# A bound on the gathers in flight: each waits for the landing of the one two places ahead

## The chip, the cores and the metric

The kernel runs on one core of a Trainium2 chip. The metric is the device time of one execution in microseconds (us); less is better. The core's engines each run an instruction stream of their own: PE (TensorE, with PEld for its weight loads), DVE (VectorE), ACT (ScalarE), POOL (GpSimd) and SP (SyncE), which here only issues DMAs. They meet on semaphores.

## The reference, cut to what matters

Four layers run one after another on a stream of 4 images of 48 x 48 tokens with 128 channels. The change lies in layer 1, a deformable convolution: each token looks at nine taps, each at a place that is computed from the data, and each tap is a weighted sum of four neighbouring tokens.

```python
offsets = conv3x3(x_normalized, offset_w) + offset_b          # 2 x 9 per token
y0, x0 = floor(py), floor(px); wy, wx = py - y0, px - x0        # py, px: place of each tap
val = (gather(y0, x0) * (1 - wy) * (1 - wx) + gather(y0, x0 + 1) * (1 - wy) * wx
       + gather(y0 + 1, x0) * wy * (1 - wx) + gather(y0 + 1, x0 + 1) * wy * wx)
out = einsum('bhwkc,kcf->bhwf', val, kernel.reshape(9, C, F)) + bias
```

Layer 2 (linear attention, then a choice of two among eight experts), layer 0 ahead of them (a selective scan) and layer 3 behind (attention, spectral filters) are not touched.

## The kernel before

`layers12` runs layer 1 for all four images and, woven into it, layer 2 for the first images: while the tiles of one image are convolved, the image before it goes through attention and the one before that through the experts. The stream lies in SBUF; an image is `TB` = 18 tiles of 128 tokens, and there are `NTILE` = 72 tiles.

For each image a table in HBM, `neighbours_b`, holds for every place the four neighbouring tokens side by side, 512 floats a row. SP stores these rows (line 991) when PE and ACT have turned an image's normalized channels into tokens, eight DMAs in each of eight of an image's 18 tile times, one image ahead of their use; so in the tile times of the first three images. DVE makes the row numbers `idx` of all 18 x 9 taps of an image at once (line 1055).

The path of one tile n is this. POOL issues nine indirect DMAs (line 1249), one for each tap (`TAPS` = 9): each takes 128 rows of 2 KB, 256 KB, into `G[:, g]`, where `g = n % GB` is one of `GB` = 3 buffers. POOL issues the nine of a tile in a row, without looking at their landing. Ahead of a tile's first gather it waits for `s_bank`: PE must have used the buffer up, three tiles earlier; ahead of an image's first it also waits for the table and the row numbers. Each gather adds 16 to the one semaphore of its buffer, `s_gat[g]`, when it lands. DVE (`weight`, line 1092) waits until all nine of the tile have landed, then multiplies `G` with the corner weights in two parts, three taps and six. PE (`turn`, line 1297) turns the 36 blocks and adds up the four corners of each tap, ACT copies the sums out of PSUM (line 1422), and PE (`convolve`, line 1315) multiplies them with the kernel.

The order is written by hand, tile by tile, the same on each engine. In the turn of tile n, DVE weighs the first part of tile n + 1, does its share of preparing the next image, then a round of layer 2, then the second part of tile n + 1 and a second round. PE turns tile n, lays a round of layer 2, convolves tile n and lays a second round. POOL has nothing but the gathers in this stage.

Of the kernel before, what the change touches and what calls it, by code (L numbers as in the profile page):

```python
# [840 lines left out]
TAPS = 9  # L841
IW = WW + 4
GB = 3
# [11 lines left out]
def layers12(nc, x_in, w, wa, wm, tables):  # L855

    with ExitStack() as ctx:
# [3 lines left out]
        sem = Semaphores(nc, ctx, "l12_")  # L861
# [43 lines left out]
        s_bank, s_wd, s_ev, s_out, s_res, s_wp = (sem(n) for n in (  # L905
            "sum_bank", "weighted", "summed_copied", "out_made", "residual", "weights_spread"))
        s_xs = [sem(f"rows_stored_{r}") for r in range(XR)]
        s_gat = [sem(f"gathered_{r}") for r in range(GB)]
        s_lp, s_ld, s_hp, s_hd, s_sq, s_ln, s_rs, s_kb, s_kn, s_ke, s_qn, s_qe, s_vs, s_mx, s_e, s_st, s_wc, s_dl, s_dr, s_cm = (sem(n) for n in (
            "round_laid", "round_taken", "half_laid", "half_weighted", "squared", "log_var", "rstd", "k_biased", "k_negative", "k_exp",  # L910
            "q_negative", "q_exp", "quotient_step", "logits_centred", "logits_exp", "choice_step", "mix_weights", "den_log", "den_inverse", "centring_made"))
# [44 lines left out]
        with nc.Block() as block:  # L956
# [38 lines left out]
            def _(dve):  # L995
# [77 lines left out]
                def spread(b, half):  # L1073
                    a, f = (t[:, half * HT:(half + 1) * HT].rearrange("p n (k t) -> p n k t", t=2) for t in (near, far))
                    dve.wait_ge(s_idx, b + 1)
                    if b or half:
                        dve.wait_ge(s_wd, 2 * (b * TB + half * HT))
                    for q in range(4):
                        dve.tensor_tensor(W4[:, :, :, q:q + 1], (f, a)[q // 2][:, :, :, 0:1], (f, a)[q % 2][:, :, :, 1:2],
                                          ALU.mult).then_inc(s_wp, 1)  # L1080

                def weight(n, part):

                    g = n % GB
                    if part == 0:
                        if n % HT == 0:
                            spread(n // TB, n // HT % 2)
                            dve.wait_ge(s_wp, 4 * (n // HT + 1))
                        dve.wait_ge(s_gat[g], (n // GB + 1) * TAPS * 16)
                    taps = (tap_banks[0], range(3, TAPS))[part]  # L1090
                    cols = slice(4 * taps[0], 4 * taps[-1] + 4)
                    dve.tensor_tensor(G[:, g, cols], G[:, g, cols],  # L1092
                                      W4[:, n % HT].rearrange("p k q -> p (k q)")[:, cols].unsqueeze(2).broadcast_to([P, 4 * len(taps), C]),
                                      ALU.mult).then_inc(s_wd, 1)
# [121 lines left out]
                for part in range(2):  # L1216
                    weight(0, part)
                dve.wait_ge(s_w2, 16 * len(loads2))
                dve.tensor_tensor(cmat[:], ident[:], ones_c[:], ALU.subtract).then_inc(s_cm, 1)
                for n in range(NTILE):  # L1220
                    k = 2 * (n - TB)
                    if n + 1 < NTILE:
                        weight(n + 1, 0)
                    if n // TB + 1 < NB:
                        prepare(n // TB + 1, n % TB)
                    if n >= TB:
                        take(k)
                        weigh_half(k)
                    if n + 1 < NTILE:
                        weight(n + 1, 1)  # L1230
                    if n >= TB:
                        take(k + 1)
                        weigh_half(k + 1)
                take(NRD - 1)

            @block.gpsimd
            def _(pool):
                for n in range(NTILE):
                    b, g = n // TB, n % GB
                    if n == 0:  # L1240
                        pool.wait_ge(s_zd, 16 * 16 * NB)
                    if n % TB == 0:
                        for r in range(XR):
                            pool.wait_ge(s_xs[r], 16 * 8 * len(range(r, (b + 1) * NPR, XR)))
                        pool.wait_ge(s_idx, b + 1)
                    if n >= GB:
                        pool.wait_ge(s_bank, NBK * (n - GB + 1))
                    for k in range(TAPS):
                        pool.indirect_dma_start(out=G[:, g, 4 * k:4 * k + 4, :].rearrange("p q c -> p (q c)"), out_offset=None,  # L1249
                                                in_=tables[b], in_offset=bass.IndirectOffsetOnAxis(ap=idx[:, b % 2, n % TB, k:k + 1], axis=0),  # L1250
                                                ).then_inc(s_gat[g], 16)

            @block.tensor
            def _(pe):
# [1432 lines left out]
def program(nc, w, x_in, out, scratch):  # L2687

    with nc.sbuf_tensor("eps", [P, 2], F32) as eps, nc.semaphore("eps_loaded") as s_eps, \
            nc.psum_tensor("psum", [P, 8 * BANK], F32) as psum:  # L2690
        with nc.Block() as block:
            @block.sync
            def _(sp):
                sp.dma_start(eps[:], w["eps"]).then_inc(s_eps, 16)
                sp.wait_ge(s_eps, 16)

        def part(prefix):

            own = {k[len(prefix):]: v for k, v in w.items() if k.startswith(prefix)}
            return {**w, **own, "eps5": eps[:, 0:1], "psum": psum}  # L2700

        x1, _, _, f_scr = scratch
        c_rows = nc.dram_tensor("c_rows", (2, NS, RC), F32, kind="Internal").ap()
        back_rows = nc.dram_tensor("back_rows", (KD // 2, NRC, KEPT, RC), F32, kind="Internal").ap()
        layer0(nc, x_in, part("l0_"), x1, c_rows, back_rows)

        with nc.sbuf_tensor("stream", [P, NT], F32) as stream:
            w["stream"] = stream
            tables = [nc.dram_tensor(f"neighbours_{b}", (QW * QW, 4 * C), F32, kind="Internal").ap() for b in range(NB)]
            layers12(nc, x1, part("l1_"), part("la_"), part("mo_"), tables)  # L2710
            layer2_attention(nc, part("la_"), NB - 1)
            layer2_experts(nc, part("mo_"), (NB - 2, NB - 1))
            layer3_attention(nc, part("ca_"))
            f_sum = nc.dram_tensor("filter_sums", (2, KF * 2, SETS * SETW), F16, kind="Internal").ap()
            layer3_spectral(nc, part("st_"), f_scr, f_sum.rearrange("o k (g x) -> o k g x", g=SETS), out)
# [24 lines left out]
```

## Time and profile before

| | us |
|---|---|
| runs, median of 3 (least, most) | 7853.32 (7848.3, 7858.25) |
| the profiled execution | 7834.9 |
| its span, first to last instruction | 7833.1 |
| from the first gather's issue to DVE's start on the last tile | 3915.05 to 4786.21 |

The profile is of one execution; its numbers add up to its own span, which is 0.2% under the median of the runs. Busy time is what an engine's instructions take; the time that an instruction of POOL takes to issue a DMA is counted as busy there, the transfer is not. A wait is put down to what came true last. "Landing" of a DMA is counted from the start of its issue.

### The profile page before, as it was taken

The numbers are of one execution on the slowest core, as the hardware profiler recorded it, in microseconds if no ns is written. First come the engines' busy times: TensorE is split into PE (matmuls) and PEld (weight loads), VectorE is DVE, ScalarE is ACT, GpSimd is POOL, SyncE is SP. The second block draws the span as 40 slices with busy tenths as digits, with TensorE's granted clock in tenths as the row PEclk, the third lists the DMA queues.
The fourth block names the chain that finished last, engine by engine and source line by source line (L and its number), as shares of the span: only waits on it lengthen the run. The fifth ranks groups of instructions, "written<-read, shape, count | busy, mean of one in ns | idle before, by whom it ended". The sixth has DMA issues, their size and how long they took to land. (4 is left out here: it accounts for less than half of the span.)

```text
span 7833.1 us, 167005 instructions
## 1 busy us (share of the span) xinstructions
PE 6962.2 (89%) x61178; PEld 6072.3 (78%) x61178; DVE 5887.2 (75%) x8892; ACT 4277.6 (55%) x9069; POOL 3533.3 (45%) x2869
## 2 busy tenths in 40 slices
PE   8999899998999989999668998899789889899898
PEld 6888678886788867888468785466588888889888
DVE  7899888997889978899557775555566666666666
ACT  6888678985789848898313332254522222222222
POOL 5888558884688837888277663200000000000000
PEclk9999999999999999999789999899899999999999
DMA  2333223332233313333377763000033333333333
GB/s 67 94 96 98 76 69 94 96 96 64 81 93 97 96 53 93 91 99 97 111 232 232 203 192 91 3 1 0 9 117 114 112 111 111 118 111 111 101 111 99
DMA packets 593198, 771.58 MB, mean 99 GB/s; under 512 B 51175, under 2 KB 530536, under 8 KB 590225
## 3 DMA queue, kind: packets, MB, share of 16 engines
q1 hardware_dynamic: 540561, 590.63, 25.3%
q0 software_dynamic: 51840, 169.91, 7.4%
q8 instruction: 551, 9.03, 0.5%
q14 instruction: 246, 2.02, 0.1%
HBM read 724.84 MB, written 35.50 MB: 97 GB/s over the span
## 5 line engine op out<-in xcount | busy, mean ns | idle before, releaser
L684 POOL TENSOR_TENSOR l_arena<-l_arena 128x768 f32<-128x768 f32 x1536 | 2574.3, 1687 | 490.1 <-DVE l_arena L614 399.6
L614 DVE TENSOR_TENSOR_SCAN l_arena<-l_arena,psum 128x772 f32<-128x772 f32 x1536 | 2647.6, 1748 | 169.5 <-PE psum L440 142.3
L535 ACT ACTIVATE l_arena<-l_arena,l_A 128x384 f32<-128x384 f32 x3072 | 1652.2, 602 | 2.1 <-DVE l_arena L584 2.1
L440 PE MATMUL psum<-l_arena 128*128 128x128 f32 x9216 | 1219.8, 283 | 154.6 <-DVE l_arena L614 145.4
L440 PEld LDWEIGHTS psum<-l_arena 128*128 128x128 f32 x9216 | 1111.8, 195 | 302.6 <-issue 287.9
L451 PE MATMUL psum<-l_ident,l_arena 128*128 128x128 f32 x9216 | 1267.7, 274 | 69.6 <-ACT l_yT L541 43.2
L451 PEld LDWEIGHTS psum<-l_ident,l_arena 128*128 128x128 f32 x9216 | 1060.6, 142 | 90.7 <-issue 53.2
L525 ACT ACTIVATE l_arena<-l_arena,l_BT 128x256 f32<-128x256 f32 x2304 | 997.0, 496 | 50.9 <-PE psum L438 37.8
L2307 POOL TENSOR_TENSOR st_mab<-st_xr 128x384 f32<-128x384 f32 x8 | 7.8, 998 | 2214.0 <-DVE st_xr L2297 2214.0
L2582 ACT ACTIVATE st_own_s<-psum 128x384 f32<-128x384 f32 x256 | 125.5, 490 | 1315.3 <-PE psum L2419 1194.8
L1249 POOL DMA_INDIRECT l_G<-neighbours,l_idx x648 | 620.7, 958 | 390.9 <-issue 189.5
L438 PE MATMUL psum<-l_ident,l_arena 128*128 128x128 f32 x4608 | 639.0, 275 | 0.9
L2419 PE MATMUL psum<-st_FS,st_xt 128*128 128x128 f16 x6912 | 536.4, 222 | 95.7 <-issue 94.4
L438 PEld LDWEIGHTS psum<-l_ident,l_arena 128*128 128x128 f32 x4608 | 523.4, 141 | 94.2 <-issue 55.4
L2419 PEld LDWEIGHTS psum<-st_FS,st_xt 128*128 128x128 f16 x6912 | 448.6, 99 | 117.9 <-issue 100.7
L2409 PE MATMUL psum<-st_F,st_xt 128*128 128x128 f16 x4608 | 434.0, 221 | 56.5 <-issue 56.5
L2439 PE MATMUL psum<-st_Uc,st_Wm 128*128 128x128 f32 (+1 forms) x2560 | 463.9, 313 | 6.4 <-DVE st_Uc L2559 6.4
L1092 DVE TENSOR_TENSOR l_G<-l_G,psum 128x1536 f32<-128x1536 f32 (+1 forms) x144 | 366.2, 2547 | 116.5 <-DMA l_G<-neighbours,l_idx 116.0
L591 DVE TENSOR_TENSOR l_arena<-psum,l_BT 128x384 f32<-128x384 f32 x768 | 409.8, 534 | 0.0
L1297 PE MATMUL psum<-l_ident,l_G 128*128 128x128 f32 x2592 | 317.6, 283 | 65.0 <-DVE l_G L1092 37.5
L2439 PEld LDWEIGHTS psum<-st_Uc,st_Wm 128*128 128x128 f32 x2560 | 364.2, 196 | 7.5 <-DVE st_Uc L2559 7.5
L1297 PEld LDWEIGHTS psum<-l_ident,l_G 128*128 128x128 f32 x2592 | 302.1, 146 | 87.6 <-DVE l_G L1092 43.6
(435 smaller groups left out, 10950.0 us busy)
## 6 DMA issues: line engine op xcount, KB each, us to landing
st_FS<-filter_sums SPq DMA_DIRECT2D x128, 1155.0 KB, 9.1
l_arena<-c_rows SPq DMA_DIRECT2D x768, 192.0 KB, 3.0
l_arena<-back_rows SPq DMA_DIRECT2D x768, 192.0 KB, 3.1
st_F<-filter_parts SPq DMA_DIRECT2D x128, 320.5 KB, 6.8
neighbours<-l_xt SPq DMA_DIRECT2D x256, 72.0 KB
st_mab<-in_st_mp SPq DMA_DIRECT2D x68, 256.0 KB, 9.2
st_mab<-in_st_mm SPq DMA_DIRECT2D x68, 256.0 KB, 6.8
l_G<-neighbours,l_idx POOLq DMA_INDIRECT x648, 3.7
```

The costliest lines, as they stand in the source:

```text
L438: mm = pe.transpose(ps[:, o:o + P], xT[:, rank[s] % 2, t, h * P:(h + 1) * P], ident[:])
L440: mm = pe.matmul(ps[:, o:o + P], dtuT[:, g % 2, t, h * P:(h + 1) * P], diagB[:, rank[s] % 3, t, :], start=True, stop=True)
L451: mm = pe.matmul(y_ps[:, t, h * P:(h + 1) * P], hC[:, s % NHC, h, t * P:(t + 1) * P], ident[:], start=(n == 0 and h == 0 and t % 2 == 0), ...
L525: ins = act.activation(xT[:, i % 2, t, :], dtuT[:, g % 2, t, :], ACT.Copy, scale=BT[:, g % 2, t, n:n + 1])
L535: act.activation(decay[:, s % NDC, half(h)], dtv[:, g % 2, h, :], ACT.Exp, scale=A[:, g // NRC, h, n:n + 1]).then_inc(s_exp, 1)
L614: dve.tensor_tensor_scan(hbuf[:, n, run], decay[:, s % NDC, run], x2_ps[s % 2][:, run], 0.0, ALU.mult, ALU.add).then_inc(s_scan, 1)
L684: pool.tensor_tensor(hC[:, s % NHC], halves(hbuf[:, s % NS, :]), Cs[:, s % NCS, :].unsqueeze(1).broadcast_to([P, 2, RC]), ALU.mult).then_i ...
L1249: pool.indirect_dma_start(out=G[:, g, 4 * k:4 * k + 4, :].rearrange("p q c -> p (q c)"), out_offset=None, in_=tables[b], in_offset=bass.In ...
L1297: mm = pe.matmul(bank(i % 2, P * a, P * (a + 1)), G[:, g, 4 * k + q, :], ident[:], start=(q == 0), stop=(q == 3), is_transpose=True, skip_ ...
L2409: mm = pe.matmul(ps[:, LOW + i * P:LOW + (i + 1) * P], xt[:, xpart, blk, :], tap[:, r, fpart, z, shift + at:shift + at + P], start=(n + m ...
L2419: mm = pe.matmul(ps[:, at + i * P:at + (i + 1) * P], xt[:, xpart, x0 + LB - 1 - i, :], FS[:, r, fpart, z, three, shift + i * P:shift + (i ...
L2439: mm = pe.matmul(ps[:, o:o + hi - lo], Wm[:, r, z, m, :], src[:, lo - c * RC:hi - c * RC], start=False, stop=False, skip_group_check=True)
```

## The change

The nine gathers of a tile are split by parity over two semaphores: the taps 0, 2, 4, 6, 8 of a buffer add to `s_gat[g][0]`, the taps 1, 3, 5, 7 to `s_gat[g][1]`. Ahead of tap k, from the third on, POOL waits until tap k - 2 has landed. The first two taps of a tile wait for no landing, as before. DVE's weighting of a tile now waits for both semaphores of the buffer, each at its own count (five gathers and four). The order of the instructions on all engines stays; three more semaphores are cleared at the end of the stage.

```diff
-        s_gat = [sem(f"gathered_{r}") for r in range(GB)]
+        s_gat = [[sem(f"gathered_{r}_{e}") for e in range(2)] for r in range(GB)]
+        OF_TILE = (TAPS - TAPS // 2, TAPS // 2)
...
-                        dve.wait_ge(s_gat[g], (n // GB + 1) * TAPS * 16)
+                        for e in range(2):
+                            dve.wait_ge(s_gat[g][e], (n // GB + 1) * OF_TILE[e] * 16)
...
                     for k in range(TAPS):
+                        if k >= 2:
+                            pool.wait_ge(s_gat[g][k % 2], (n // GB * OF_TILE[k % 2] + k // 2) * 16)
                         pool.indirect_dma_start(out=G[:, g, 4 * k:4 * k + 4, :].rearrange("p q c -> p (q c)"), out_offset=None,
                                                 in_=tables[b], in_offset=bass.IndirectOffsetOnAxis(ap=idx[:, b % 2, n % TB, k:k + 1], axis=0),
-                                                ).then_inc(s_gat[g], 16)
+                                                ).then_inc(s_gat[g][k % 2], 16)
```

On POOL, the start of the stage before: 27 gathers of three tiles with one wait at their head, then the first gather of the fourth tile, which waits for PE (`l12_sum_bank`), and eight more.

```order
L1236 UNCONDITIONAL_BRANCH [waits barrier_Pool_Activation_PE_DVE_SP_gather]
L1249 DMA l_G<-neighbours,l_idx 128x512 [waits l12_rows_stored_2,l12_rows_stored_1,l12_indices_made,l12_rows_stored_0,l12_border_zeroed]
L1249 DMA l_G<-neighbours,l_idx 128x512 x26
L1249 DMA l_G<-neighbours,l_idx 128x512 [waits l12_sum_bank]
L1249 DMA l_G<-neighbours,l_idx 128x512 x8
```

The same place now (`l12_gathered_0_1` is buffer 0, odd taps), the first tile's last two gathers and on into the second tile; the rows left out by "..." go on in the same alternation:

```order
L1253 DMA l_G<-neighbours,l_idx 128x512 [waits l12_rows_stored_2,l12_rows_stored_1,l12_indices_made,l12_rows_stored_0,l12_border_zeroed]
L1253 DMA l_G<-neighbours,l_idx 128x512
L1253 DMA l_G<-neighbours,l_idx 128x512 [waits l12_gathered_0_0]
L1253 DMA l_G<-neighbours,l_idx 128x512 [waits l12_gathered_0_1]
...
L1253 DMA l_G<-neighbours,l_idx 128x512 x2
L1253 DMA l_G<-neighbours,l_idx 128x512 [waits l12_gathered_1_0]
L1253 DMA l_G<-neighbours,l_idx 128x512 [waits l12_gathered_1_1]
```

No gather has moved; seven of a tile's nine have a wait that they hadn't, and the two that follow each other without one (`x2`) are the first two of the next tile.

On DVE, at the third and fourth tile, before: the weighting of a tile's first three taps waits for the buffer's one semaphore.

```order
L1092 TENSOR_TENSOR l_G<-l_G,psum 128x1536 [waits l12_gathered_2]
L1010 COPY l_gst<-psum 128x2 [waits l12_gn_group]
L1011 TENSOR_TENSOR l_gst<-l_gst 128x1 [waits l12_dve_a]
L1012 TENSOR_TENSOR l_gst<-l_gst 128x1 [waits l12_dve_a]
L1092 TENSOR_TENSOR l_G<-l_G,psum 128x3072
L1092 TENSOR_TENSOR l_G<-l_G,psum 128x1536 [waits l12_gathered_0]
```

And now:

```order
L1094 TENSOR_TENSOR l_G<-l_G,psum 128x1536 [waits l12_gathered_2_1,l12_gathered_2_0]
L1011 COPY l_gst<-psum 128x2 [waits l12_gn_group]
L1012 TENSOR_TENSOR l_gst<-l_gst 128x1 [waits l12_dve_a]
L1013 TENSOR_TENSOR l_gst<-l_gst 128x1 [waits l12_dve_a]
L1094 TENSOR_TENSOR l_G<-l_G,psum 128x3072
L1094 TENSOR_TENSOR l_G<-l_G,psum 128x1536 [waits l12_gathered_0_1,l12_gathered_0_0]
```

The instructions stand as they stood; the first part of each weighting waits for two semaphores in place of one.

## Rows read from the trace of the kernel before

**Rows 1.** The page's busy times, and POOL in 40 slices of the span.

```profile
PE 6962.2 (89%) x61178; PEld 6072.3 (78%) x61178; DVE 5887.2 (75%) x8892; ACT 4277.6 (55%) x9069; POOL 3533.3 (45%) x2869
POOL 5888558884688837888277663200000000000000
```

**Rows 2.** Busy time by stretch (us): stretch, length, engines, clock, DMA share, GB/s.

```profile
3770.00:3914.00 144.00, 82.09 (x272) 46.69 (x272) 67.31 (x121) 24.23 (x37) 1.86 (x2) 0.69 0.39 122
3914.00:4136.00 222.00, 152.11 (x1108) 140.76 (x1109) 118.58 (x102) 37.40 (x82) 167.64 (x176) 0.85 0.78 227
4136.00:4352.00 216.00, 194.32 (x1406) 176.40 (x1404) 159.31 (x227) 80.78 (x206) 163.60 (x171) 0.96 0.78 229
4352.00:4570.00 218.00, 214.04 (x1432) 178.19 (x1432) 159.78 (x244) 75.88 (x201) 140.18 (x146) 0.98 0.69 198
4570.00:4800.00 230.00, 228.24 (x1597) 192.44 (x1596) 162.21 (x226) 70.25 (x180) 149.31 (x157) 1.00 0.63 182
```

**Rows 3.** Waits, 3914 to 4790: us in total, times, longest.

```profile
POOL l_G L1249 <- issue: 189.5, 622, 0.3
...
DVE l_G L1092 <- DMA l_G<-neighbours,l_idx: 116.0, 29, 14.0
POOL l_G L1249 <- PE psum L1297: 58.2, 25, 4.6
```

**Rows 4.** Timeline, 3913.8 to 3918: start, length, operation, [idle before, releaser].

```profile
3913.91 0.25 DVE L1055 CAST l_idx<-l_low 128x162 uint32<-128x162 f32 x1
...
3915.05 1.15 POOL L1249 DMA_INDIRECT l_G<-neighbours,l_idx  x1 [143.19 <-DVE l_idx L1055]
3916.51 0.95 POOL L1249 DMA_INDIRECT l_G<-neighbours,l_idx  x1 [0.30 <-issue]
3917.76 0.95 POOL L1249 DMA_INDIRECT l_G<-neighbours,l_idx  x1 [0.30 <-issue]
```

**Rows 5.** Line 1092 alone in the third stretch: DVE's busy time (instructions).

```profile
4352.00:4570.00 218.00, 79.80 (x32) 0.98 0.69 198
```

**Rows 6.** Line 1249, whole stage: ns min/median/max, starts; then landing times, us.

```profile
L1249 POOL DMA_INDIRECT l_G<-neighbours,l_idx x648: 940/946/2398, 3915.1 to 4782.5; - x162
...
DMA to landing us min/median/max: 3.1/3.7/5.2
```

**Rows 7.** Timelines of POOL, PE and ACT about 4420, a tile that waits for PE.

```profile
4418.84 0.94 POOL L1249 DMA_INDIRECT l_G<-neighbours,l_idx  x1 [0.30 <-issue]
4420.07 4.09 PE L1297 MATMUL psum<-l_ident,l_G 128*128 128x128 f32 x36
4424.20 0.49 ACT L1422 ACTIVATE l_val<-psum 128x384 f32<-128x384 f32 x1 [0.82 <-PE psum L1297]
4424.43 0.94 POOL L1249 DMA_INDIRECT l_G<-neighbours,l_idx  x1 [4.65 <-PE psum L1297]
```

**Rows 8.** Line 1249: one lone, nine after rest, nine with stores, first stretch.

```profile
L1249 POOL DMA_INDIRECT l_G<-neighbours,l_idx x1: 940/940/940, 4424.4 to 4424.4; - x1
...
DMA to landing us min/median/max: 3.4/3.4/3.4
L1249 POOL DMA_INDIRECT l_G<-neighbours,l_idx x9: 942/946/948, 4700.6 to 4710.6; - x9
...
DMA to landing us min/median/max: 3.3/3.6/3.8
L1249 POOL DMA_INDIRECT l_G<-neighbours,l_idx x9: 946/946/1160, 4200.0 to 4210.3; - x9
...
DMA to landing us min/median/max: 3.6/4.4/5.0
DMA to landing us min/median/max: 3.4/3.8/5.2
```

**Rows 9.** DVE's timeline at the end of the stage.

```profile
4786.21 1.75 DVE L1092 TENSOR_TENSOR l_G<-l_G,psum 128x1536 f32<-128x1536 f32 x1 [1.53 <-DMA l_G<-neighbours,l_idx]
4789.09 0.29 DVE L1177 TENSOR_TENSOR stream<-stream,psum 128x128 f32<-128x128 f32 x1 [1.12 <-PE psum L1344]
...
4809.95 0.27 DVE L1579 MEMSET la_vv<- 128x258 f32 x1 [3.93 <-PEq L55]
```

## The prediction

> **What bounds the kernel now.** The change lies in one stage, so I first looked for what paces that stage. The totals of the page and its slices say little of it: over the whole span PE is busy 89% and POOL 45%, and POOL's busy slices from the 20th to the 25th are the stage of layers 1 and 2 [rows 1]. The busy time by stretch, one stretch for each image, says more [rows 2]. In the first two stretches POOL is busy 167.64 of 222 us and 163.60 of 216 us, and PE only 152.11 and 194.32. To POOL's busy time its own gaps are to be added: in the waits of the stage, 622 of the 648 gathers have "issue" time ahead of them, 189.5 us in all, 0.30 us each [rows 3]. 176 gathers of 0.95 us and as many gaps of 0.30 make 220 of the first stretch's 222 us: POOL issues without a pause there, 1.25 us from one gather to the next [rows 4], 11.25 us for a tile of nine. In the third and fourth stretch POOL rests, 58.2 us in all, until PE has used up a buffer [rows 3], and PE is busy 214 of 218 and 228 of 230 us [rows 2]: PE paces those. The 32 weightings of the third stretch [rows 5], two a tile, make 16 tiles of 13.6 us. Over all 72 tiles the stage runs from 3915.05, its first gather, to 4786.21, when DVE gets the last one [rows 4, 9]. That is 12.1 us a tile.
>
> Then I asked how long one gather takes from its issue to its landing, since the change makes that a link of a chain. The line's own answer gives 3.1 / 3.7 / 5.2 us as least, median and greatest [rows 6]. At one issue each 1.25 us, 3.7 us means that about three gathers are in flight now (3.7 / 1.25 = 2.96). Two is therefore fewer than the kernel uses at present, on the very engine that paces half of the stage.
>
> **The change part by part.**
>
> *The semaphores.* Three more of them are cleared behind the stage. Between DVE's last operation there and its first in the next stage lie 3.93 us of idle time [rows 9], which hold the clearing of the stage's semaphores among other things (51 instructions in the program's order); three more can cost at most 3 x 3.93 / 51 = 0.2 us. DVE's second wait per tile comes true before or with the first, because the ninth gather, the last to be issued, counts on the semaphore that DVE waits for first. Its price is under the 0.04 us by which an engine starts after its releaser (ACT, below), on an engine that has idle time at each tile. I book both as nothing, 0.2 us if I am wrong.
>
> *The waits on POOL.* Gathers 3 to 9 of each tile wait for the landing of the gather two places ahead, 7 x 72 = 504 waits. Queued behind the waiting instruction is all of POOL's later work, which in this stage is gathers alone; SP's stores of neighbour rows stand in another queue. Who waits for POOL is DVE's weighting of the tile, and behind DVE the PE transposes; DVE's waits for gathers are 116.0 us now [rows 3], and they are what will grow.
>
> The length of a link is the time to landing, L, and the step from the landing to the next issue, h. No row shows a POOL instruction released by a landing. The nearest show it released by PE: a tile's 36 transposes run from 4420.07 for 4.09 us, to 4424.16; ACT, waiting for the same, starts at 4424.20, POOL at 4424.43 [rows 7]. So h is 0.27 on POOL, where ACT needs 0.04. It is also the 0.30 of the gap between gathers, so I read it as POOL's own start-up, paid after the release. The other end is the first gather of the stage, 0.89 us after the cast that it waited for ended (3914.16 to 3915.05, [rows 4]); that is one start after 143 us of rest with several waits. I take 0.28.
>
> For L there are four rows. A gather that POOL issued after 4.65 us of rest, when the gathers ahead had landed, took 3.4 [rows 7, 8]. Of nine issued from 4700.6 on, behind a shorter rest, the fastest took 3.3, the median 3.6 [rows 8]. The least of all is 3.1 [rows 6]. Where SP stores rows the median of nine is 4.4 [rows 8]; that touches 8 of 18 tiles in three images. With two in flight a gather is less alone than the 3.4 and less crowded than the median of 3.7, so I take 3.55, midway, and keep 3.1 and the 3.8 of the crowded first stretch [rows 8] as ends.
>
> The odd-numbered gathers carry the tile: gathers 1, 3, 5, 7 and 9 follow each other at L + h = 3.83 us. The even ones start 1.25 us behind and reach no further (1.25 + 3 x 3.83 = 12.74 for the eighth, and 1.25 more is 13.99, before the ninth's 15.32). The next tile's first gather waits for no landing, so it follows the ninth at 1.25. The pace of a tile becomes 4 x 3.83 + 1.25 = **16.57 us** in place of 11.25.
>
> That is above the 13.6 us of a PE-paced tile, so the gathers set the pace in all 72 tiles, and a wait for a free buffer goes away (the three buffers are then used up long before they are wanted). Of the 5.32 us that a tile gains, what the PE-paced stretches already took is not paid again; I therefore sum by end times, not by adding to each tile. The last tile's first gather starts at 3915.05 + 71 x 16.57 = 5091.5, its ninth 15.3 later at 5106.8, and it lands at 5110.4. Now DVE gets it at 4786.2 [rows 9]. Difference: **+324 us**. Behind it the tail is the same work, less the 1.12 us that DVE there waits for a PE that is late [rows 9] and then isn't. Sum: +323 us.
>
> The profiled execution took 7834.9 us (span 7833.1), the median of the runs is 7853.3, 0.2% more. I add the sum to the median: **8176 us**; on the profiled run it would be 8158.
>
> Ends: L = 3.1 gives 14.77 us a tile and +193 by the same sum, L = 3.8 gives 17.57 and +395. That is 8046 to 8249.
>
> A rule that speaks of L, in sentences that the sum does not need. The rows show the landing to depend on what else moves: 3.4 us alone, 4.4 among SP's stores [rows 8]. The Trainium skill, "DMA: Bandwidth & Descriptors", section "Latency and other measured facts", says that less load on HBM makes the fixed part of a DMA smaller. By the rows alone the sum is +323; by that rule it would go towards the +193 of the least landing, since two gathers load less than three.
>
> **The rivals.**
>
> *Not slower: the landings get short enough.* What must hold is a tile of 12.1 us, the stage's present mean: (12.1 - 1.25) / 4 - 0.28 = 2.43 us for L. Then the pauses on POOL only fill what it rests now for buffers, and the time stays at 7853. For it speaks that a third of the traffic in flight goes; the stage's DMA share is 0.63 to 0.78 [rows 2], so queues may stand. Against it speaks the lone gather, 3.4 us with nothing ahead of it, and that not one of the recorded landings is under 3.1. Chance 2%. Anything faster than before needs an L below that and a gain besides; 1%.
>
> *The landings shrink to between 2.5 and 3.1 us.* A weaker form of the same: 2.5 gives 12.37 us a tile, +20 and 7873; 2.6 gives 12.77, +49 and 7902; 3.1 ends at 8046. It takes a landing faster than any recorded. Chance 5%. (The Trainium skill, same page, "Anatomy of one DMA — SWDGE (gpsimd) path", fits a DMA as 2.0 us and its bytes over 436 GB/s; for a gather's 256 KB that is an estimate of 2.6 us. The lone gather's 3.4 us [rows 8] agrees only if the 0.95 us of issuing come on top, which makes 3.55.)
>
> *Slow starts on POOL.* If a start after a landing costs 0.89 rather than 0.28, a tile takes 4 x 4.44 + 1.25 = 19.0 us, the sum is +499 and the time 8352. Against it: POOL started 0.27 us after its releaser from a rest of 4.65 us [rows 7], and the new rests are shorter than that. Chance 5%, and 3% for landings that stay above 3.8 for another reason (stores that spread).
>
> *PE's clock becomes the bound.* PE rests more, and the granted clock could fall: it was 0.85, a mean between its levels of 1.2 and 2.4 GHz, in the stretch where PE was busy 69% [rows 2]. In the third stretch PE has 214.04 / 16 = 13.4 us a tile at 0.98; it would take over from 16.57 at a clock of 0.79. PE would still be busy about 80%, more than where 0.85 was granted, so I don't expect it. At 0.69, the lowest of the stretch before the stage [rows 2], those 16 tiles would take 19.0 us, +39 us, 8215. Chance 3%, and inside the range.
>
> **How the numbers follow.** The forecast, gathers as the pace of all tiles with L between 3.1 and 3.8, has 81%. The range 8046 to 8250 holds it and the clock's case, 84% in all; the other four rivals and a time under 7837 make the 16% outside. Measurements of this kernel tell 0.2%, some 16 us, from no change: faster 1%, within that 2%, slower 97%.
>
> **What would show it.** POOL's starts of line 1253 in pairs, 1.25 to 1.5 us and then about 2.4 us, with 3.83 us from one to the next but one; a tile's first gathers 16.57 us apart in all four images; POOL's waits for PE gone and waits for landings in their place, some 2.3 us for every second gather; DVE's wait for gathers at about 72 x 5 us; PE's busy share under 80% in the stage. The rest of the kernel, before 3915 and behind the stage, should be the same to a microsecond. Wrong would be: landings under 2.5 us, or starts on POOL that come 0.9 us behind a landing.

## The result, and the profile after

The changed kernel took 8165.87 us (median of 4 runs, 8156.31 to 8166.18), the kernel before 7851.43 in the runs beside it: a ratio of 1.0396, 95% interval 1.0378 to 1.0414. That is 314 us slower; 8176 was forecast, and the forecast range was 8046 to 8250. The profiled execution took 8166.18 us, its span is 8164.4.

The busy time by stretch answers to [rows 2], again one stretch for each image (stretch, length, then PE, PEld, DVE, ACT and POOL busy, granted clock, DMA share, GB/s):

```profile
3916.00:4213.00 297.00, 165.49 (x1044) 152.86 (x1044) 108.30 (x89) 35.55 (x78) 155.11 (x163) 0.76 0.57 159
4213.00:4514.00 301.00, 212.01 (x1352) 194.96 (x1352) 150.09 (x208) 79.29 (x200) 154.97 (x163) 0.84 0.56 158
4514.00:4816.00 302.00, 256.60 (x1609) 212.44 (x1610) 176.80 (x272) 82.49 (x215) 155.34 (x162) 0.90 0.56 157
4816.00:5110.00 294.00, 236.59 (x1480) 192.96 (x1478) 153.37 (x214) 67.39 (x172) 153.68 (x163) 0.91 0.51 146
```

From each image's first gather to the next one's, the four images took 204.5, 205.5, 239.0 and 218.5 us before (the last one up to its last gather), the first two paced by POOL and the others by PE. The stretches of [rows 2] are cut a little otherwise, the first two hold 176 and 171 gathers in place of 162. Counted the same way the images now take 296.6, 301.0, 302.7 and 289.9 us, whatever else they hold: one thing paces them all. POOL's busy time is what it was, some 155 us an image on the mean, so POOL issues the same work with longer rests. The traffic fell from 227 to 159 GB/s in the first stretch.

What the rests are is said by the gathers' own line, which answers to [rows 3, 6] (the idle time of POOL ahead of the line by what ended it, in us and times; then who waited for the line; then landing times):

```profile
L1253 POOL DMA_INDIRECT l_G<-neighbours,l_idx x648: 940/944/2369, 3916.1 to 5106.3; - x162
its engine sat idle before it (us, times) until:
  DMA l_G<-neighbours,l_idx: 502.4, 458
  DVE l_idx L1056: 143.4, 1
  issue: 68.2, 184
  PE psum L1301: 1.5, 5
who waited for it (us, times):
  DVE l_G L1094: 561.9, 72
...
DMA to landing us min/median/max: 3.1/3.4/6.2
```

POOL's waits for a free buffer, 58.2 us before, are 1.5 us now: the buffers lie ready. In their place stand 502.4 us of waits for landings. DVE waits for every one of the 72 tiles. And the landing itself has become quicker at the median, 3.4 us for 3.7, with fewer gathers side by side.

The chain is seen gather by gather in POOL's timeline of the first tile, which answers to [rows 4]:

```profile
3916.10 1.15 POOL L1253 DMA_INDIRECT l_G<-neighbours,l_idx  x1 [143.36 <-DVE l_idx L1056]
3917.56 0.95 POOL L1253 DMA_INDIRECT l_G<-neighbours,l_idx  x1 [0.30 <-issue]
3919.78 0.94 POOL L1253 DMA_INDIRECT l_G<-neighbours,l_idx  x1 [1.27 <-DMA l_G<-neighbours,l_idx]
3921.09 0.94 POOL L1253 DMA_INDIRECT l_G<-neighbours,l_idx  x1 [0.37 <-DMA l_G<-neighbours,l_idx]
3923.29 0.94 POOL L1253 DMA_INDIRECT l_G<-neighbours,l_idx  x1 [1.26 <-DMA l_G<-neighbours,l_idx]
...
3930.47 0.94 POOL L1253 DMA_INDIRECT l_G<-neighbours,l_idx  x1 [1.27 <-DMA l_G<-neighbours,l_idx]
3931.72 0.95 POOL L1253 DMA_INDIRECT l_G<-neighbours,l_idx  x1 [0.30 <-issue]
3932.97 0.95 POOL L1253 DMA_INDIRECT l_G<-neighbours,l_idx  x1 [0.30 <-issue]
```

The third gather starts 3.68 us after the first, the fifth 3.51 after the third, the ninth 14.37 after the first, and the next tile's first two follow at 1.25 us each without a wait. From the first gather to the last one's start, 3916.1 to 5106.3, lie 72 tiles less that last step, so a tile takes (1190.2 + 1.25) / 72 = 16.55 us, and a link of the chain (16.55 - 1.25) / 4 = 3.82.

The end of the stage on DVE answers to [rows 9]:

```profile
5109.58 1.75 DVE L1094 TENSOR_TENSOR l_G<-l_G,psum 128x1536 f32<-128x1536 f32 x1 [9.13 <-DMA l_G<-neighbours,l_idx]
5111.25 0.28 DVE L1179 TENSOR_TENSOR stream<-stream,psum 128x128 f32<-128x128 f32 x1
...
5131.75 0.27 DVE L1583 MEMSET la_vv<- 128x258 f32 x1 [4.43 <-PEq L55]
```

From the first gather to DVE's start on the last tile the stage takes 1193.5 us, 871.2 before: +322.3. The tail behind it takes 22.2 us for 23.7. The stretch from there to the end took 3032.7 us and 3023.2 in the two profiled executions; in the run with the semaphores split and no wait (below), where that code is the same, it took 3037. So the spans' difference of 331 us is 321 from the stage and its tail, 1 ahead of it, and the rest is how executions differ behind it.

### The profile page after: what moved, and what is told of

It reads as the page before. It is cut to its first block and busy times, and to the rows that moved or that the text cites. A ratio compares the mean times of both kernels' runs of the same rounds, so it can differ in the third digit from the quotient of the medians.

```text
span 8164.4 us, 167068 instructions
## 1 busy us (share of the span) xinstructions
PE 7063.5 (87%) x61174; PEld 6150.2 (75%) x61178; DVE 5886.7 (72%) x8892; ACT 4281.8 (52%) x9069; POOL 3532.0 (43%) x2869
## 3 DMA queue, kind: packets, MB, share of 16 engines
q0 software_dynamic: 51840, 169.91, 7.4%
## 5 line engine op out<-in xcount | busy, mean ns | idle before, releaser
L1253 POOL DMA_INDIRECT l_G<-neighbours,l_idx x648 | 619.1, 955 | 715.4 <-DMA l_G<-neighbours,l_idx 502.4
L1094 DVE TENSOR_TENSOR l_G<-l_G,psum 128x1536 f32<-128x1536 f32 (+1 forms) x144 | 366.7, 2550 | 562.2 <-DMA l_G<-neighbours,l_idx 561.9
L1301 PE MATMUL psum<-l_ident,l_G 128*128 128x128 f32 x2592 | 343.8, 297 | 108.5 <-DVE l_G L1094 79.5
L1301 PEld LDWEIGHTS psum<-l_ident,l_G 128*128 128x128 f32 x2592 | 329.4, 156 | 138.5 <-DVE l_G L1094 87.4
```

What stands on the lines that cost most here:

```text
L1301: mm = pe.matmul(bank(i % 2, P * a, P * (a + 1)), G[:, g, 4 * k + q, :], ident[:], start=(q == 0), stop=(q == 3), is_transpose=True, skip_ ...
```

## The experiments

Theory: the landing time is now a link of a chain, and a tile takes four links and one issue. Rival 1: each of the 504 waits costs POOL a fixed time, 314 / 504 = 0.62 us. Rival 2: it is the split of the semaphores, and DVE's second wait.

**The split alone.**

```diff
-                        if k >= 2:
-                            pool.wait_ge(s_gat[g][k % 2], (n // GB * OF_TILE[k % 2] + k // 2) * 16)
```

> The two semaphores a buffer and DVE's two waits stay, POOL's 504 waits are taken out. Theory (the chain of landings paces the gathers: a tile takes 4 links of landing time plus start, 4 x 3.83 + 1.25 us): without the chain the time is that of the kernel before, 7851 within 16 us. Rival 1 (each wait on POOL costs about 314 / 504 = 0.62 us whatever it waits for): 7851 too. Rival 2 (the split of the semaphores and DVE's second wait cost the time): stays at 8166.

Measured: 7859.82 us beside 7846.55, ratio 1.0013 (1.0003 to 1.0023). POOL's rests in that run are those of [rows 3], 189.5 us of issue and 58.3 us for PE. Rival 2 falls, for all but 0.1%. Most of that tenth lies outside the stage: from its first gather to its last the profiled executions take 868.4 us here and 867.5 before. What the rest is stays open. By its design this run can't tell rival 1 from the theory; the next two can.

**One in flight.** One semaphore a buffer, and each gather waits for the one ahead of it:

```diff
-                        if k >= 2:
-                            pool.wait_ge(s_gat[g][k % 2], (n // GB * OF_TILE[k % 2] + k // 2) * 16)
+                        if k >= 1:
+                            pool.wait_ge(s_gat[g][k % 1], (n // GB * OF_TILE[k % 1] + k // 1) * 16)
```

> Each gather of a tile waits for the one ahead of it, one semaphore a buffer. Theory: eight links of 3.35 + 0.28 and one issue of 1.25 make 30.3 us a tile; over 71 tiles and the last one's nine gathers the stage ends 1312 us later than before: about 9160. Rival 1: 576 waits at 0.62 us, +357, 8208.

Measured: 9163.16 us, one run. Rival 1 is out by 955 us. POOL's timeline in the middle of the stage shows single links, and below it the landing times of the run:

```profile
4501.19 0.94 POOL L1253 DMA_INDIRECT l_G<-neighbours,l_idx  x1 [2.56 <-DMA l_G<-neighbours,l_idx]
4504.76 0.94 POOL L1253 DMA_INDIRECT l_G<-neighbours,l_idx  x1 [2.63 <-DMA l_G<-neighbours,l_idx]
4508.38 0.95 POOL L1253 DMA_INDIRECT l_G<-neighbours,l_idx  x1 [2.68 <-DMA l_G<-neighbours,l_idx]
4511.94 0.95 POOL L1253 DMA_INDIRECT l_G<-neighbours,l_idx  x1 [2.61 <-DMA l_G<-neighbours,l_idx]
...
DMA to landing us min/median/max: 3.2/3.3/4.5
```

Starts lie 3.57, 3.62 and 3.56 us apart, the median landing is 3.3. Taken gather by gather from the trace, POOL starts 0.26 us after the landing that it waited for (570 waits, 0.258 to 0.260), as it did after PE [rows 7], and not 0.89 as at the stage's first start. The sum, 9160, is 3 us off.

**Three in flight.** Three semaphores a buffer, and each gather waits for the one three places ahead:

```diff
-                        if k >= 2:
-                            pool.wait_ge(s_gat[g][k % 2], (n // GB * OF_TILE[k % 2] + k // 2) * 16)
+                        if k >= 3:
+                            pool.wait_ge(s_gat[g][k % 3], (n // GB * OF_TILE[k % 3] + k // 3) * 16)
```

> Each gather waits for the one three places ahead in its tile, on three semaphores in turn: 432 waits in place of 504. Theory: gathers 1, 4, 7 make a chain of two links of 3.7 + 0.28 = 3.98 us where three issues take 3.75, so a tile goes from 11.25 to about 11.7 us, paid only in the two image times that POOL paces, 36 tiles: about 16 us more than before, 7867, and some more where rows are stored; under 7900. Rival 1 (0.62 us for each wait): 432 x 0.62 = 268 us, 8119.

Measured: 7903.49 us beside 7846.55, ratio 1.0068 (1.0051 to 1.0085): +57 us. Rival 1's 8119 is out here too. The theory's sign is right, its size isn't: 16 us were expected, and under 7900. The gathers' line says where the rest is:

```profile
its engine sat idle before it (us, times) until:
  DMA l_G<-neighbours,l_idx: 169.0, 280
...
DMA to landing us min/median/max: 3.1/3.7/7.8
```

From image to image the stage grew by 29, 31, 0 and 5 us. So the wait is paid where the theory had it, in the two images that POOL paces, but at 1.6 to 1.7 us a tile. Two links at the median, 2 x (3.7 + 0.28), are only 0.46 us over the six issues between, but 280 of the 432 waits held POOL up, for 0.6 us each. Without a bound, a landing of 5 us delays nothing as long as the tile's last one isn't late. With three there is no slack at all (3.98 against 3.75 us), so a slow landing holds up what follows, and a quick one afterwards gives nothing back. I had reckoned with the median. The mean landing of these two images, 4.0 us, gives 1.06 us a tile by the same sum, 38 us in all. That the rest comes from the spread too, since POOL issues the three chains in one order and a late landing in one holds up the others, is the likely reading; no run shows it apart.

**The bound over the tile's edge.** In the changed kernel the first two gathers of a tile wait for no landing; here they do:

```diff
+                        elif n:
+                            pool.wait_ge(s_gat[(n - 1) % GB][1 - k], ((n - 1) // GB + 1) * OF_TILE[1 - k] * 16)
```

> As the changed kernel, but the first two gathers of a tile wait for the last two but one place of the tile ahead too: never more than two in flight. Theory: nine links make two tiles, 4.5 links a tile in place of 4 and an issue of 1.25; at 3.4 + 0.28 that is 16.56 us a tile, at 3.6 + 0.28 (rows stored) 17.46: 0 to 64 us above the changed kernel, about 8185. The first gather's landing, 3.5 us and more in the changed kernel, comes down to that of the others, 3.4. Rival 1: 142 waits more at 0.62 us, +88, 8254.

Measured: 8223.96 us (8213.53 to 8229.79), ratio to before 1.0473 (1.0456 to 1.0491), 58 us above the changed kernel. From first to last start its 647 steps take 1.92 us each, 3.84 a link and 17.28 a tile, 0.73 more than the changed kernel: 71 x 0.73 = 52. That is the upper half of what the theory gave, and 30 us under rival 1's. A tile's first two gathers land after 3.3 and 3.4 us at the median, where they took 3.6 and 3.7 in the changed kernel: that much of their landing came from the crowd at the tile's edge.

**No later stores.** SP stores the first image's rows alone, before the stage's first gather:

```diff
-                for b in range(NB):
+                for b in range(1):
                     for m in range(NPR):
...
-                            pool.wait_ge(s_xs[r], 16 * 8 * len(range(r, (b + 1) * NPR, XR)))
+                            pool.wait_ge(s_xs[r], 16 * 8 * len(range(r, NPR, XR)))
...
-                                                in_=tables[b], in_offset=...
+                                                in_=tables[0], in_offset=...
...
-                        act.wait_ge(s_xs[g % XR], 16 * 8 * (g // XR))
+                        act.wait_ge(s_xs[g % XR], 16 * 8 * min(g // XR, len(range(g % XR, NPR, XR))))
```

> The changed kernel, but SP stores neighbour rows of the first image alone, ahead of the stage's gathers, and all 72 tiles take their rows from that table; so the output is that of other rows for three images. The 24 tiles that had stores beside them in the changed kernel have none. Theory (landing times pace, and what stretches them is SP's stores): every tile goes at the pace of those that had none, 15.8 us in the changed kernel's trace, in place of 16.56 on the mean: 71 x 0.76 = 54 us less, 8112. Rival (the pace does not hang on what else the DMA engines do): 8166.

Measured: 8147.75 us (8146.79 to 8149.99), beside 8173.98 for the changed kernel and 7845.16 for the kernel before on the same chip:

> The changed kernel once more, on the chip of the two runs beside it: 8166 within 16 us by every theory.

That is 26 us less, half of the 54 expected. Stores do stretch the chain (a tile takes 16.13 us for 16.56), but not all of its slow tiles go with them. Tiles of 17 to 19 us remain, among others at the places 23, 34, 40, 66 and 67 in both kernels. The 54 was also too much from the start. In the changed kernel's trace 15.8 us is the pace of the tiles that have neither stores nor, as the next run brings up, a packet of instructions beside them. All its 47 tiles without stores took 16.18 us on the mean, the 24 with stores 17.31; those 24 x 1.13 = 27 us are about what went.

**Mirrored rows.** The run before, with one edit:

```diff
-                                                ...IndirectOffsetOnAxis(ap=idx[:, b % 2, n % TB, k:k + 1], axis=0),
+                                                ...IndirectOffsetOnAxis(ap=idx[:, b % 2, TB - 1 - n % TB, k:k + 1], axis=0),
```

> The run without later stores, with the tiles of an image taking their rows in the opposite order (tile 18b + s gathers what tile 18b + 17 - s gathered), so the output differs once more. In the traces of the changed kernel and without later stores the tiles 23, 34, 40, 66 and 67 (from 0) are slow in every run, 17.3 to 19 us against a median near 16. Theory A (the rows that they ask for are slow to read): the slow tiles move to their mirror places 30, 19, 49, 59 and 58. Theory B (something else at that place of the program, such as fetches of instructions that use the same DMA engines): they stay where they are. The time is that of the run without later stores, 8148 within 16 us, by both.

Measured: 8144.57 us, one run. The slow tiles stayed: 18.85 us at place 23, 17.54 at 40, 17.23 at 66 and 18.35 at 67 (34 fell to 16.69), and their mirror places 19, 30, 49 and 58 took 15.4 to 16.4. The fifth mirror place, 59, took 17.17, but 17.09 before the mirroring too. So it is not the rows. POOL's timeline of tile 67, and then the DMA queues in its 18.35 us and in the 15.6 us of the tile behind it (packets, MB, share of 16 engines):

```profile
5001.09 0.95 POOL L1253 DMA_INDIRECT l_G<-neighbours,l_idx  x1 [0.30 <-issue]
5002.34 0.95 POOL L1253 DMA_INDIRECT l_G<-neighbours,l_idx  x1 [0.30 <-issue]
5004.86 0.94 POOL L1253 DMA_INDIRECT l_G<-neighbours,l_idx  x1 [1.57 <-DMA l_G<-neighbours,l_idx]
5007.15 0.94 POOL L1253 DMA_INDIRECT l_G<-neighbours,l_idx  x1 [1.35 <-DMA l_G<-neighbours,l_idx]
5009.86 0.95 POOL L1253 DMA_INDIRECT l_G<-neighbours,l_idx  x1 [1.76 <-issue]
...
q0 software_dynamic: 720, 2.36, 43.4%
q8 instruction: 1, 0.02, 0.5%
q14 instruction: 1, 0.01, 0.1%
...
q0 software_dynamic: 720, 2.36, 51.6%
```

The slow tile has packets of the queues named instruction in it, the quick one has none. Counted the same way for the 71 tiles that another follows, from one tile's first gather to the next one's: 28 tiles without a packet of queue q8 take 15.7 us on the mean, 43 with one take 16.35. In the run without later stores it is 28 at 15.8 and 43 at 16.4. Those 43 x 0.6 = 26 us are what was missing from the expected 54. In part POOL itself stands: the 1.76 us ahead of the fifth gather are put down to nothing that the profile shows. Such stands come at fixed places, eleven tiles apart: ahead of the sixth gather of tile 12 and of the fifth of tiles 23, 34, 45, 56 and 67, in every run with two in flight. Three of them in the run without later stores (tiles 23, 34 and 56):

```profile
4304.07 0.94 POOL L1253 DMA_INDIRECT l_G<-neighbours,l_idx  x1 [2.75 <-issue]
...
4482.59 0.94 POOL L1253 DMA_INDIRECT l_G<-neighbours,l_idx  x1 [2.59 <-issue]
...
4837.68 0.94 POOL L1253 DMA_INDIRECT l_G<-neighbours,l_idx  x1 [2.81 <-issue]
```

With one in flight they are 4.05 to 4.85 us long; before the change and with the split alone no gap put down to "issue" is over 0.3. Besides, in the tiles 4, 22 and 40 the issue of a gather or two takes 1.5 to 2.8 us in place of 0.95, before the change as after it. In the run without later stores eight of the 43 tiles with a packet have such a stand or such an issue and take 17.6 us on the mean, the other 35 take 16.1. So some 14 of the 26 us lie in the tiles where POOL stands, the rest in small parts in the others. That the packets cause both, the slow landings and the stands, is argued from their meeting in the same tiles; no run took them away, and why POOL stands at these places stays open.

**Half rows.** Gathers of 1 KB a row:

```diff
-                        pool.indirect_dma_start(out=G[:, g, 4 * k:4 * k + 4, :]..., 
-                                                in_=tables[b], ...
+                        pool.indirect_dma_start(out=G[:, g, 4 * k:4 * k + 2, :]...,
+                                                in_=tables[b].rearrange("r (h c) -> (r h) c", h=2), ...
```

> The changed kernel with gathers of 1 KB a row in place of 2 KB: two of each tap's four neighbours, and from other rows, so the output differs; the other half of the buffer is set to zero once at the start of the stage. The packets of a gather took 14.3 us of engine time in the trace of before (7.4% of 16 engines' span over 648 gathers), 0.9 us on 16 engines. Theory with the landing made of bytes in good part: 0.45 us less a link, 4 x 0.45 = 1.8 us a tile, 8166 - 127 = 8039. Rival (the landing is a fixed time, bytes hardly count): 8166, or up to 14 us more for the zeroing.

Measured: 7979.09 us (7978.24 to 7988.43), 195 us under the changed kernel beside it, more than either side expected.

```profile
L1254 POOL DMA_INDIRECT l_G<-neighbours,l_idx x648: 940/944/1854, 3915.7 to 4921.6; - x162
...
DMA to landing us min/median/max: 2.5/2.8/4.7
```

The issue takes the same 944 ns, the landing 2.8 us for 3.4. A tile takes (1005.9 + 1.25) / 72 = 13.99 us, 2.57 less, 0.64 a link. So the landing isn't a fixed time: half the bytes are worth 0.64 us, where the packets' time on the DMA engines gave 0.45. That two gathers share the engines explains little of it, since a gather of 2 KB rows alone in flight still takes 3.3 us. With the bytes the packets are fewer too (the gathers' queue has 31104 for 51840, and 84.98 MB for 169.91), and the rows lie elsewhere; the run does not tell bytes from packets.

## Why the prediction was right, point by point

- **What bounds the stage.** Right. The chain paces all four images alike, and the waits for a free buffer went, 58.2 to 1.5 us. The 13.6 us of a PE-paced tile came from a stretch that isn't quite an image; the third image took 239.0 / 18 = 13.3. Nothing hung on it.
- **The link.** 3.83 us foreseen, 3.82 measured; the tile 16.57 and 16.55; the stage +324 and +322.3; the tail -1.1 and -1.5. The start after a landing, read from a start after PE as 0.28, is 0.26 in the runs with one and with two in flight. The step from PE as a releaser to a DMA as one was the least sure of the sum, and it held.
- **The landing, 3.55 us.** Right on the mean, by a wrong picture, so in good part by luck. I took one value between lone and crowded. What came is 3.3 to 3.4 us for most gathers, so that a tile without stores or instruction packets takes about 15.8 us, and a tail up to 6.2 us that pulls the mean up: gathers behind a tile's edge, where up to four are in flight, gathers beside stores, and tiles with instruction packets. Two of the three, and POOL's own stands, I had not counted or named. The rule of the Trainium skill, "DMA: Bandwidth & Descriptors", section "Latency and other measured facts", that a lighter load makes the fixed part smaller, agrees with the median, 3.7 to 3.4 us; its consequence, a time well under the sum, did not come, because the tail stayed.
- **The even gathers reach no further.** Right as a rule, but they start mostly 1.3 to 1.6 us behind, not 1.25, and once in 72 tiles the ninth gather follows the eighth at once instead of waiting for the seventh's landing.
- **Split semaphores, nothing.** 0.13% (0.03 to 0.23), at the bound of what can be told. The idle time behind the stage that holds the clearing went from 3.93 to 4.43 us, with the split alone as well: 0.5 us for three semaphores, where I had put 0.2 as the most.
- **What would show it.** POOL's rests were foreseen as 2.3 us for every second gather; they are about 1.3 and 0.5 us in turn. The 2.3 was a slip: the steps of about 2.4 us beside it leave 1.45 behind an issue of 0.95. DVE's waits were put at 360 us and are 561.9: DVE's waits in the stage that PE ended fell from 129.6 to 14.1 us, and that time now ends with a landing. PE was to be busy under 80%: over the stage it is 73%, in the third stretch 85%. The code behind the stage was to take the same to a microsecond; it took 9.5 us more, and 13.8 more with the split alone, so it can't be told that well.
- **The clock.** That rival went some of the way: the granted clock, a mean between the levels of 1.2 and 2.4 GHz, fell from 0.98 to 0.90 in the third stretch and from 0.85 to 0.76 in the first, where PE rested most. PE still had 45 us to spare in the third. With POOL's waits for PE at 1.5 us it cost the stage nothing that shows.
- **Not slower.** It needed landings of 2.43 us; only with half the bytes did they come near, 2.8, and even then the time was 1.0175 times that of before.

The terms erred by 1 to 2 us, and the sum by 10: 8176 for 8166. The difference is of the size by which this kernel's executions differ outside the stage. On the chip of the last experiments the same two kernels lie 329 us apart (8173.98 and 7845.16, ratio 1.0416), so the +323 stands between the two measurements, 314 and 329.

## What to carry to other kernels

A bound on transfers in flight turns each landing into a link of a chain. Its price is read from three rows: the landing time of a lone transfer, the engine's start after a release, and the pace of issue now. If the bound times the pace of issue is less than landing plus start, the chain paces, and the sum is to be made with the mean landing, not the median: with a tight bound slow landings are paid and quick ones give nothing back. Where the bound just balances landing plus start, even the mean gives too little (three in flight cost 57 us where the median gave 16 and the mean 38). Sum it by the end times of the stage, so that what another engine paced there isn't counted twice.

## What the runs showed of the hardware

- A gather's landing hangs on its bytes, or on the packets that go with them, more than the packets' time says: 128 KB less made a link 0.64 us shorter, about 200 GB/s within one gather. The Trainium skill, "DMA: Bandwidth & Descriptors", section "Anatomy of one DMA — SWDGE (gpsimd) path", has bytes over 436 GB/s, which would be an estimate of 0.30 us for the half; the measurement decides, for gathers of 1 and 2 KB rows.
- Packets of the instruction queues, one in 43 of 71 tiles, go with 0.6 us more a tile when POOL waits for landings two places ahead; part of it is POOL's own stands. Before the change, in the 36 tiles that POOL paced, tiles with such a packet and tiles without took the same 11.39 us on the mean.
- POOL starts 0.26 us after the landing that it waits for. With such waits it also stands 1.6 us and more at fixed places, 98 or 99 gathers apart, without a releaser in the profile; without them it doesn't.
